# The current step's tap of a Mamba convolution moves from VectorE to ScalarE, which computes it with its bias out of PSUM, in a four-block decoder kernel on one core

## The chip, the cores and the metric

The kernel runs on one core of a Trainium2 chip. The metric is the device time of one launch in microseconds (us). A core has five engines that run programs of their own and wait for each other on semaphores: TensorE (PE in the profile, with its weight loads as PEld), VectorE (DVE), ScalarE (ACT), GpSimd (POOL) and SyncE (SP, which starts DMAs).

## The reference, cut to what matters

32 samples of 128 tokens and 256 features go through four blocks: an attention, a Mamba-2 block with a cross attention, a masked decoder layer and an attention with a feed-forward part. The change lies in the Mamba block's causal convolution of four taps over time, for each of 768 channels:

```python
zxbcdt = _rms(x, norm_w) @ in_proj_w
z = zxbcdt[..., :D_INNER]
xBC = zxbcdt[..., D_INNER:D_INNER + CONV_DIM]
...
padded = jnp.pad(xBC, ((0, 0), (D_CONV - 1, 0), (0, 0)))
conv = conv_b + sum((padded[:, k:k + L, :] * conv_w[:, k] for k in range(D_CONV)))
xBC = jax.nn.silu(conv)
```

Tap 3 is that of the current step: it reads the unshifted values.

## The kernel before, in words

One sample after another goes through a list of some 100 named tasks (xbc0, Q3, scores1, ...). Each engine has its own order of all tasks of all samples, sorted from a table of places written out by hand (TASKS, FIRST, LAST, SETUP, SHIFT), so that each engine works on up to five samples in turn: while one sample is in its Mamba block, others are in later attentions. "Xbc0 of sample 13" is written xbc0(13) here; samples count from 0. An engine never takes a later task while an earlier one waits.

Channels lie on the 128 partitions for the convolution: 768 channels are six chunks of 128 channels by 128 steps. The way of a sample through it:

- PE: the tasks xbc0 and xbc1 each project three chunks into one PSUM bank (in `xbc`, through `to_channels`, L639).
- ACT: `xbc` (L1104) copies the bank, 128x384, into the SBUF tile raw behind three columns of zeros, and then frees the bank.
- DVE: `convolve` (tasks conv0 and conv1) waits until the copy is done, then writes conv = raw x tap 3 + bias, three instructions (L1353), and adds taps 0, 1 and 2, nine instructions (L1358). Between taps it waits on a semaphore of its own (`step`), since each tap reads what the last one wrote.
- ACT: `convolved` (task silu, L1118) takes the tanh of conv/2 over all six chunks; DVE `silu` (L1364) gives x times sigmoid; PE `pairs` (L843, then transposes at L627) multiplies the B and C chunks and turns the others. DVE then scans (L1392), masks (L1396), and PE goes on in task Y (L858).

Four PSUM banks form a ring. Each PE task that writes one (a job: xbc0, x3T, mT4, K3, Q3 and so on) claims the next bank in PE's order: job number modulo 4. `claim` makes PE wait until the job four places earlier has been read, which the reading engine tells through bank_read. Another four banks, score, hold attention scores.

Around the convolution PE's order in most samples is: row(n-2), xbc0(n), x3T(n-2), mT4(n-3), quads1(n-1), K3(n-2), Q3(n-2), z1(n), xbc1(n), quads3(n-2), turn1(n-1), V3(n-2), e3(n-2), values1(n-1), ... , z0(n), values4(n-3), x2T(n-1), ld(n), quadsT3(n-2), pairs(n). Row, x3T, mT4, K3, Q3, z1 use the ring, quads1 does not. So xbc0's bank is the one that Q3 claims. ACT's order there is x3T (L1019), row (L1149), xbc0 (L1104), scores1 (eight exponentials, L1044), Q3 (L1025), z1 (L1111 to L1113), xbc1 (L1104), softplus (L1099), turn1 (two copies, L1057). DVE's is scores1 (L1249), K3 (L1465), conv0, scores3, e3, softplus (L1372 to L1374), finish1, n3, conv1, mT3 (L1269), Wo (L1432 to L1436), silu (L1364).

SPARE gives numbers of idle matmuls (L634) that PE runs ahead of some tasks of the first samples, where it would otherwise stand still. A spare one shows as two matmuls in the trace. ACT work with a scale or a bias that is a column of values, one for each partition, is `nc.scalar.activation(..., scale=..., bias=...)`.

Of the kernel before, what the change touches and what calls it, by code (L numbers as in the profile page):

```python
# [9 lines left out]
ALU = mybir.AluOpType  # L10
ACT = mybir.ActivationFunctionType
AX_X = mybir.AxisListType.X

P = 128
# [10 lines left out]
TAPS = 4  # L25
# [27 lines left out]
    back2=42.7145, back3=51.1225, back4=64.1374, conv0=15.1721, conv1=-1.5314, ctxT=34.1467, decayed=32.8056, down=71.1144,  # L53
# [20 lines left out]
    Y=(-0.1446, -0.2213, 0, -0.2465, 0, -0.2111, -0.4731, -0.2058), am=(-0.7507, 0, 0.1238, 0.0772, 0.1122, 0.0313, 0.0705, 0),  # L74
# [3 lines left out]
    back2=(-0.3118, -0.5887, -0.1007, 0.1753, 0.4363, 0.188, -0.0778, -0.0163),  # L78
# [17 lines left out]
    ld=(-1.9618, -0.6167, -0.8394, 0.0345, 0.9095, 0.0199, 0.0318, -0.0664),  # L96
    loadc=(-0.1305, -2.114, 0, -0.1491, 0, -0.1671, 0.0566, -1.6471),
    loadx=(-1.0589, 1.7209, 0.3386, -1.5237, 2.0519, -0.0978, 2.0094, -0.9573),
    mT2=(-0.2214, -0.039, 0, -0.1666, -0.0082, -0.1469, 0, 0), mT3=(0.1507, -0.0649, 0, 0.0742, 0.0046, -0.0294, -0.0199, 0),
    mT4=(0.0725, -0.0808, 0.0206, 0, 0.298, -0.0486, 0.0939, 0), n2=(0, -0.3557, 0, 0.1358, 0, 0.0553, -0.089, -0.9991),  # L100
    n3=(0.0571, 0.1417, 0.0077, 0, 0, 0.0336, -0.0298, -0.0179), norm2=(0, 0, 0.0986, 0.039, 0.0839, -0.1068, 0, -0.0236),
    norm3=(0.2169, 0, 0.1959, 0, -0.0031, 0, 0.0318, 0.324), norm4=(0.071, 0.0335, 0.32, -0.1077, 0.2364, -0.0289, 0.096, 0.0302),
    norm5=(0.0068, -0.3911, 0.0867, 0, 0.5488, -0.0845, 0, -0.0979),
    pairs=(-0.1812, 0.017, 0.1446, 0.0111, -0.0547, 0.0181, -0.0375, 0),
# [27 lines left out]
    xhatT=(-0.6957, 0.4202, 0.4868, 0, -0.2191, -0.364, 0.188, -0.0647),  # L132
    xnT=(-0.1522, 0, 0.002, -0.142, -0.1203, -0.0386, 0.273, -0.0477),
# [13 lines left out]
    back2=(0.1938, 0.0024, 0.135, -0.005, -0.0551, -0.2771), back3=(0.0375, -0.032, -0.245, -0.0948, 0.0736, 0.6035),  # L147
# [9 lines left out]
    ld=(0.0029, -0.2246, 0.1986, 0, 0.0376, 0.1683), loadc=(3.1754, 0, -0.3153, 0, 0, 0),  # L157
# [5 lines left out]
    pairs=(-0.0772, 0.1328, 0.0556, -0.01, 0.2526, 0.0232), proj=(0.0701, 0, -0.0083, 0.4015, 0, 0.3376),  # L163
# [9 lines left out]
    uT=(0, -0.1254, 0.2253, 0, -0.135, 0.0359), up0=(-0.1023, -0.0508, 0.2482, -0.1079, -0.8006, 27.5814),  # L173
# [8 lines left out]
    xnT=(0.032, -0.0811, 0.0628, -0.074, -0.0236, -0.0959), z0=(0.032, 0, -0.0425, 0.0328, 0, -0.0819),  # L182
# [8 lines left out]
    ACT=dict(  # L191
        K2=0.4275, K4=0.371, KE2=2.1051, KE3=-8.3627, Q1=0.2401, Q2=0.4113, Q3=0.0246, Q4=1.2096, V1=0.0661, V2=0.6553, V3=0.3112,
        Y=1.0681, attT2=-3.4331, attT3=31.0217, attT4=8.7138, ctxT=-0.4571, exps2=-6.4438, exps3=39.9244, exps4=40.2808,
        fc1=0.7372, ld=-0.1039, row=0.2044, scores1=-0.7902, silu=-0.1882, softplus=-0.2365, turn1=0.1793, uT=0.4762, up0=0.6797,
        up1=0.4246, x1=-0.5175, x2T=-0.0673, x3T=0.071, x4T=0.2522, x5T=0.318, x6T=0.3578, xbc0=0.1868, xbc1=0.439, xhatT=0.0635,
        xnT=0.9282, z0=0.0015, z1=0.2322, K0=-24.9607, Q0=-31.7526, V0=-0.7018, attT0=-21.6729, exps0=39.9731, prep_in=-3.1006),
# [11 lines left out]
        ld=8.6234, loadc=-5.0975, loadx=16.7863, spread=13.2176, store=78.055, load_mamba=-31.3063, load_w1=-56.8981,  # L208
# [26 lines left out]
PLACE_OF = {engine: {key: n for n, key in enumerate(order)} for engine, order in ORDER.items()}  # L235


SPARE = {("mT0", 0): 11, ("values0", 0): 9, ("back0", 0): 3, ("xhatT", 0): 6, ("ld", 0): 16, ("pairs", 0): 5, ("Y", 0): 18, ("uT", 0): 6, ("xnT", 0): 9, ("ctxT", 0): 10, ("x2T", 0): 7, ("Y", 1): 3, ("mT2", 0): 4, ("back2", 0): 3, ("n3", 0): 3}


RING_JOBS = dict(bias="bias0 bias1", pairs="CB xh", turn1="turn1_0 turn1_1")
# [162 lines left out]
def decoder_stack(nc, a, out):  # L404

    ctx = ExitStack()
    with ctx:
        def sb(name, shape, dt=F32):
            return ctx.enter_context(nc.sbuf_tensor(name, shape, dt))
# [29 lines left out]
        def vec(name):  # L439
            return vectors[:, VECTOR_AT[name]:VECTOR_AT[name] + VECTORS[name]]  # L440

        m_norm, g_norm, conv_b, ca_w, ca_b = (vec(n) for n in ("m_norm", "g_norm", "conv_b", "ca_w", "ca_b"))
        conv_w = vec("conv_w").rearrange("p (c k) -> p c k", c=XBC)
# [18 lines left out]
        raw = sb("raw", [P, 2, XBC, TAPS - 1 + P])  # L462
# [23 lines left out]
        conv = sb("conv", [P, 2, XBC, P])  # L486
        dbx, dx, zs, tz = (sb(n, [P, 2, INNER]) for n in ("dbx", "dx", "zs", "tz"))
        uT = tz[:, :, :].rearrange("p m (c k) -> p m c k", c=IC)
# [112 lines left out]
        def _(pe):  # L601
# [28 lines left out]
            def spare(it, what, lane, times):  # L630

                t, full = claim(it, what, lane)
                for _ in range(times):
                    mm(t[:, 0:P], ident, ident, start=True, stop=True)  # L634
# [363 lines left out]
            def program():  # L998
                for task, l, i in ORDER["PE"]:
                    if i == 0 and (task, l) in SPARE:  # L1000
                        spare(Of(i), RING_JOBS.get(task, task).split()[0], l, SPARE[task, l])
                    if task in do:
# [5 lines left out]
        def _(act):  # L1008
            run = nc.scalar.activation

            def filled(it, what, lane=0):

                b, use = job(it, what, lane)
                act.wait_ge(bank_full[b], use + 1)
                return bank[b], bank_read[b]
# [74 lines left out]
            def copied(what, n=D):  # L1090

                return lambda it, l: copy_out(it, what, l, actT[:, l], n)
# [8 lines left out]
            def xbc(it, l, half):  # L1101
                n = XBC // 2
                t, read = filled(it, f"xbc{half}", l)
                nc.scalar.copy(raw[:, l % 2, half * n:(half + 1) * n, TAPS - 1:],  # L1104
                               t[:, 0:n * P].rearrange("p (c k) -> p c k", c=n)).then_inc(read, 1)

            def z(it, l, half):
                n = INNER // 2
# [71 lines left out]
            def up(it, l, half):  # L1180
                t, read = filled(it, f"up{half}", l)
                for k in range(FC // 2):
# [7 lines left out]
                      ld=decays, Y=Y, uT=flip_u, xnT=copied("xnT"), Q1=Q1, x2T=copied("x2T"),  # L1190
                      Q2=Q2, K2=K_2, V2=V_2, x3T=copied("x3T"), row=row, Q3=Q3, V3=V3, x4T=copied("x4T"), fc1=fc1,
                      K4=K4, x5T=copied("x5T"), Q4=Q4, x6T=copied("x6T"),
                      **{f"{task}{half}": lambda it, l, f=f, half=half: f(it, l, half)
                         for task, f in (("xbc", xbc), ("z", z), ("up", up)) for half in range(2)},
                      x1=x1)
            do.update(scores1=exponential1, turn1=turned_out1, ctxT=copied("ctxT"))
# [12 lines left out]
        def _(dve):  # L1209
            tt, ts, stt = nc.vector.tensor_tensor, nc.vector.tensor_scalar, nc.vector.scalar_tensor_tensor  # L1210
# [7 lines left out]
            def evacuated(it, what, lane=0):  # L1218
                b, use = job(it, what, lane)
                dve.wait_ge(bank_read[b], use + 1)  # L1220
# [11 lines left out]
            def normalise(it, l, root, done):  # L1232
                dve.wait_ge(S[root], nth(it, l))
                ts(att[:, l, :], res[:, l, :], stat[:, l, 0:1], stat[:, l, 10:11],
                   ALU.subtract, ALU.mult).then_inc(S[done], 1)
# [62 lines left out]
            step = Chain(dve, S["dve_first"])  # L1298
# [9 lines left out]
            def program():  # L1308
                step = Chain(dve, S["dve_step"])
# [39 lines left out]
                def convolve(l, half):  # L1349
                    chunks = range(half * XBC // 2, (half + 1) * XBC // 2)  # L1350
                    evacuated(it, f"xbc{half}", l)
                    for c in chunks:
                        last = ts(conv[:, l % 2, c, :], raw[:, l % 2, c, TAPS - 1:], conv_w[:, c, TAPS - 1:TAPS],  # L1353
                                  conv_b[:, c:c + 1], ALU.mult, ALU.add)
                    for k in range(TAPS - 1):
                        step(last)
                        for c in chunks:
                            last = stt(conv[:, l % 2, c, :], raw[:, l % 2, c, k:k + P], conv_w[:, c, k:k + 1],  # L1358
                                       conv[:, l % 2, c, :], ALU.mult, ALU.add)
                    last.then_inc(S[f"conv{half}"], 1)  # L1360
# [119 lines left out]
                def down(l):  # L1480
# [4 lines left out]

                do = dict(finish0=lambda l: weighted(it, 0, l, step, att0[:, :]), prep_in=prep_in, prep_masks=prep_masks,
                          prep_out=prep_out, prep_q1=prep_q1, K1=K_1, softplus=softplus, conv0=lambda l: convolve(l, 0), conv1=lambda l: convolve(l, 1), silu=silu, pairs=pairs, scan=scan, decayed=decayed, Y=gate,
                          uT=gate_norm, proj=mamba_out, xnT=lambda l: normalise(it, l, "rstd3", "xn"),
                          
# [202 lines left out]
```

## Time and profile before

| | us |
|---|---|
| median of 3 runs | 1672.24 (1670.99 to 1676.52) |
| the profiled execution, whole | 1675.6 |
| its span, first to last instruction | 1673.8 |
| mean granted TensorE clock | 0.99 |
| busy: PE, PEld, DVE, ACT, POOL | 1616.5, 1393.2, 1387.1, 1039.8, 493.3 |

The profile is one execution. Its busy times are unions of an engine's instructions. In lines by group, the two numbers behind the bar are the busy time in us and the mean ns of one instruction, and after the second bar stands the idle time of the engine just before them, with what ended it. In a timeline a row is start, length, engine, line, operation, written tile and read tiles, shapes and count, and in brackets the idle time before it and what ended it. Consecutive instructions of an engine overlap by some 0.1 us in these records, so starts, not lengths, tell the rate.

### The profile page before, as it was taken

Reading aid. Unit: us, or ns where it says so; the run is one execution under the profiler, and the core shown is the slowest. Engines: PE = TensorE matmul, PEld = TensorE weight load, DVE = VectorE, ACT = ScalarE, POOL = GpSimd, SP = SyncE. Lnnn points to the kernel's source line nnn. Section 1 sums busy time; section 2 is a strip of 40 time slices with the busy share of each in tenths; the row PEclk is TensorE's granted clock in tenths of the full one; section 3 lists DMA queues with packets and bytes.
Section 4 is the critical chain, followed back from the end, with each engine's and each line's share of the span. In section 5 each row is a group of like instructions: output and inputs, shape, how many; then the busy total and the mean of one; then the engine's idle time right before and its main releaser. Section 6 shows DMA issues by size and latency. Waiting matters only on the chain.

```text
span 1673.8 us, 61139 instructions
## 1 busy us (share of the span) xinstructions
PE 1616.5 (97%) x25060; PEld 1393.2 (83%) x25060; DVE 1387.1 (83%) x3585; ACT 1039.8 (62%) x2667; POOL 493.3 (29%) x1256
## 2 busy tenths in 40 slices
PE   7899999999999999999999999999999999999986
PEld 6777888888888888888888888888888888888774
DVE  4689888888888889888888988888898888898652
ACT  2355666766666676666667666666766666676652
POOL 2333223333322332332233233223323322333110
PEclk9999999999999999999999999999999999999997
DMA  6110000000000000000000000000000000000000
GB/s 216 52 64 21 6 18 31 18 25 28 22 3 24 25 24 24 25 17 9 24 25 25 25 24 22 5 24 25 24 25 24 17 10 24 21 28 19 5 5 7
DMA packets 31316, 44.37 MB, mean 27 GB/s; under 512 B 3008, under 2 KB 26176, under 8 KB 30912
## 3 DMA queue, kind: packets, MB, share of 16 engines
q1 hardware_dynamic: 31040, 40.45, 7.4%
q8 instruction: 202, 3.31, 0.8%
q14 instruction: 74, 0.61, 0.1%
HBM read 36.12 MB, written 4.33 MB: 24 GB/s over the span
## 4 chain that ended last, share of the span: by engine, by line
PE 55%; DVE 36%; issue 5%; POOL 2%; DMA 1%; ACT 1%; SPq 0%; DVEq 0%; POOLq 0%; ACTq 0%
PE ring L639 18%; PE ring L645 14%; PE ring L627 6%; DVE conv L1358 5%; DVE maxima_at L1258 5%; PE score L707 4%; DVE decay L1392 4%; PE score L731 3%; PE ring L773 3%; DVE decay L1396 2%; PE ring L858 2%; DVE conv L1364 2%; DVE QB L1269 2%; DVE conv L1353 2%; PE score L671 2%
## 5 line engine op out<-in xcount | busy, mean ns | idle before, releaser
L1533 POOL TENSOR_TENSOR stat<-stat 128x1 f32<-128x1 f32 x224 | 131.7, 594 | 617.2 <-DVE stat L1224 616.6
L1019 ACT COPY actT<-ring 128x256 f32<-128x256 f32 x256 | 95.5, 373 | 291.7 <-PE ring L627 290.5
L1258 DVE TENSOR_REDUCE maxima_at<-score 128x4 f32<-128x512 f32 x388 | 240.8, 684 | 25.5 <-PE score L707 24.5
L1052 ACT ACTIVATE weights<-score 128x512 f32<-128x512 f32 x388 | 200.7, 607 | 28.5 <-PE score L731 27.9
L1358 DVE SCALAR_TENSOR_TENSOR conv<-raw,vectors,conv 128x128 f32<-128x128 f32 x576 | 169.0, 349 | 6.8
L639 PE MATMUL ring<-actT,w_q 128*128 128x128 f32 x1024 | 141.5, 281 | 0.7 <-ACT actT L1019 0.7
L639 PEld LDWEIGHTS ring<-actT,w_q 128*128 128x128 f32 x1024 | 124.5, 191 | 12.8 <-issue 11.3
L639 PE MATMUL ring<-actT,w_up 128*128 128x128 f32 x1024 | 129.6, 281 | 0.5 <-ACT actT L1019 0.5
L639 PEld LDWEIGHTS ring<-actT,w_up 128*128 128x128 f32 x1024 | 121.1, 194 | 3.7 <-ACT actT L1019 1.1
L1184 ACT ACTIVATE gT<-ring,vectors 128x128 f32<-128x128 f32 x256 | 73.0, 368 | 72.2 <-PE ring L639 71.5
L645 PE MATMUL ring<-w_down,gT 128*128 128x256 f32 x512 | 115.9, 379 | 1.3 <-issue 1.3
L731 PE MATMUL score<-QB,KE 32*128 32x128 f32 x3104 | 115.9, 286 | 1.0 <-DVE QB L1269 1.0
L731 PEld LDWEIGHTS score<-QB,KE 32*128 32x128 f32 x3104 | 97.1, 189 | 20.7 <-issue 16.6
L773 PE MATMUL ring<-weights,V 128*32 128x128 f32 x3104 | 106.9, 278 | 3.4 <-issue 3.3
L645 PEld LDWEIGHTS ring<-w_down,gT 128*128 128x128 f32 x512 | 94.9, 190 | 13.0 <-issue 1.4
L639 PE MATMUL ring<-cT,w_k 128*128 128x128 f32 x768 | 104.4, 279 | 0.0
L1269 DVE SCALAR_TENSOR_TENSOR QB<-ring,const,QB 128x256 f32<-128x256 f32 x194 | 84.5, 477 | 20.4 <-PE ring L627 20.3
L1063 ACT COPY attT<-ring 128x512 f32<-128x512 f32 x97 | 56.2, 579 | 72.7 <-PE ring L773 72.6
L645 PE MATMUL ring<-w_v,cT 128*128 128x256 f32 x384 | 100.3, 384 | 0.4 <-ACT V L1036 0.4
L773 PEld LDWEIGHTS ring<-weights,V 128*32 128x32 f32 x3104 | 80.5, 111 | 23.8 <-issue 10.1
L639 PEld LDWEIGHTS ring<-cT,w_k 128*128 128x128 f32 x768 | 95.4, 191 | 4.9 <-issue 0.2
L639 PE MATMUL ring<-actT,w_in 128*128 128x128 f32 x768 | 98.7, 279 | 0.7 <-DVE q_bias L1337 0.7
(179 smaller groups left out, 3814.8 us busy)
## 6 DMA issues: line engine op xcount, KB each, us to landing
decay<-rates_out SPq DMA_DIRECT2D x32, 512.0 KB, 3.9
cT<-in_ctxT SPq DMA_DIRECT2D x32, 128.0 KB, 2.2
x_in<-in_x SPq DMA_DIRECT2D x32, 128.0 KB, 2.4
out<-result SPq DMA_DIRECT2D x32, 128.0 KB, 2.1
row_all<-in_rows SPq DMA_DIRECT2D x1, 1420.0 KB, 9.9
w_in<-in_in_proj SPq DMA_DIRECT2D x1, 1288.0 KB, 7.2
w_k<-in_k SPq DMA_DIRECT2D x4, 256.0 KB, 5.8
w_v<-in_v SPq DMA_DIRECT2D x4, 256.0 KB, 5.7
```

The source lines that it names most:

```text
L627: last = nc.tensor.transpose(t[:, c * P:(c + 1) * P], src[:, c * P:(c + 1) * P], ident)
L639: last = mm(t[:, at:at + P], w[:, c, cols:cols + P], xT[:, c, :], start=(c == 0), stop=(c == n - 1))
L645: last = mm(t[:, at:at + hi - lo], xT[:, c, :], w[:, c, lo:hi], start=(c == 0), stop=(c == n - 1))
L731: last = mm(score[:, r, at:at + P], KE[rows_of, l, c, e, :], QB[rows_of, l, c, e, :], start=(not masked and at == 0), stop=(c == DC - 1 an ...
L773: last = mm(output[ROWS_OF[r], four * P:(four + 1) * P], V2[:, l, h, :], weights[:, buffer, h % 8 // 2, at:at + P], start=True, stop=True)
L1019: nc.scalar.copy(dst.rearrange("p c k -> p (c k)"), t[:, 0:n]).then_inc(read, 1)
L1052: run(weights[:, turned_buffer(it, a_, l), r, :], score[:, r, :], ACT.Exp).then_inc(S["exps"], 1)
L1184: last = run(gT[:, l % 2, c, :], t[:, k * P:(k + 1) * P], ACT.Gelu, bias=up_b[:, c:c + 1])
L1258: nc.vector.tensor_reduce(maxima_at[:, maxima_buffer(it, a_, l), :, 32 * r:32 * r + 17:16], score[:, r, :].rearrange("p (c f k) -> p c f k ...
L1269: last = stt(QB[:, l, :, e, :], t[:, 0:D].rearrange("p (c k) -> p c k", c=DC), spare_row[:, e:e + 1], QB[:, l, :, e, :], ALU.mult, ALU.add)
L1358: last = stt(conv[:, l % 2, c, :], raw[:, l % 2, c, k:k + P], conv_w[:, c, k:k + 1], conv[:, l % 2, c, :], ALU.mult, ALU.add)
L1533: tt(stat[:, l, 10:11], stat[:, l, 2:3], stat[:, l, 4:5], ALU.pow).then_inc(S[done], 1)
```

## The change

ACT still copies the bank into raw. Before it frees the bank it now also computes tap 3 with its bias, with three ACTIVATEs (Identity, scale and bias both columns) for each half, from the PSUM bank straight into conv. Only the last of them frees the bank. DVE's three instructions for tap 3 are gone, and the first wait on its own semaphore with them. All engine orders are kept. Five spare matmuls of the first sample are taken away: one ahead of ld(0), four ahead of ctxT(0).

```diff
-SPARE = {... ("ld", 0): 16, ... ("ctxT", 0): 10, ...}
+SPARE = {... ("ld", 0): 15, ... ("ctxT", 0): 6, ...}
...
                 nc.scalar.copy(raw[:, l % 2, half * n:(half + 1) * n, TAPS - 1:],
-                               t[:, 0:n * P].rearrange("p (c k) -> p c k", c=n)).then_inc(read, 1)
+                               t[:, 0:n * P].rearrange("p (c k) -> p c k", c=n))
+                for k in range(n):
+                    c = half * n + k
+                    last = run(conv[:, l % 2, c, :], t[:, k * P:(k + 1) * P], ACT.Identity,
+                               scale=conv_w[:, c, TAPS - 1:TAPS], bias=conv_b[:, c:c + 1])
+                last.then_inc(read, 1)
...
                     evacuated(it, f"xbc{half}", l)
-                    for c in chunks:
-                        last = ts(conv[:, l % 2, c, :], raw[:, l % 2, c, TAPS - 1:], conv_w[:, c, TAPS - 1:TAPS],
-                                  conv_b[:, c:c + 1], ALU.mult, ALU.add)
                     for k in range(TAPS - 1):
-                        step(last)
+                        if k:
+                            step(last)
                         for c in chunks:
```

## Rows read from the trace of the kernel before

**Rows 1.** The page's first part: busy time of each engine

```profile
PE 1616.5 (97%) x25060; PEld 1393.2 (83%) x25060; DVE 1387.1 (83%) x3585; ACT 1039.8 (62%) x2667; POOL 493.3 (29%) x1256
```

**Rows 2.** Busy us (count) of PE, PEld, DVE, ACT, POOL; clock; DMA

```profile
600.00:700.00 100.00, 99.13 (x1580) 85.78 (x1581) 87.72 (x225) 65.61 (x171) 32.47 (x82) 1.00 0.07 21
```

**Rows 3.** Groups by line: the removed DVE work, the nearest ACT form

```profile
L1353 DVE TENSOR_SCALAR conv<-raw,vectors 128x128 f32<-128x128 f32 x192 | 54.5, 341 | 1.5 <-ACT raw L1104 1.5
L1176 ACT ACTIVATE QB<-ring,q_bias,const 128x128 f32<-128x128 f32 x128 | 48.3, 463 | 2.5 <-PE ring L639 2.5
```

**Rows 4.** Timeline of ACT: a train of four, then around xbc0(13) and xbc1(13)

```profile
626.39 1.51 ACT L1176 ACTIVATE QB<-ring,q_bias,const 128x128 f32<-128x128 f32 x4
...
634.41 0.37 ACT L1019 COPY actT<-ring 128x256 f32<-128x256 f32 x1 [1.04 <-PE ring L627]
...
634.83 0.50 ACT L1104 COPY raw<-ring 128x384 f32<-128x384 f32 x1
636.15 2.17 ACT L1044 ACTIVATE exps<-score,neg_max 128x128 f32<-128x128 f32 x8 [0.82 <-DVE neg_max L1249]
...
639.51 0.53 ACT L1104 COPY raw<-ring 128x384 f32<-128x384 f32 x1
640.64 0.21 ACT L1099 ACTIVATE dts<-dts 128x8 f32<-128x8 f32 x1 [0.61 <-POOL dts L1550]
641.20 0.59 ACT L1057 COPY weights<-ring 128x512 f32<-128x512 f32 x1 [0.35 <-PE ring L627]
```

**Rows 5.** Timeline of PE and of its weight loads: Q3(11) behind K3(11)

```profile
636.18 1.06 PE L639 MATMUL ring<-actT,w_q 128*128 128x128 f32 x8
...
636.08 0.97 PEld L639 LDWEIGHTS ring<-actT,w_q 128*128 128x128 f32 x8
```

**Rows 6.** Xbc0's copy of samples 9 and 31, and Q3 behind the last (window's end)

```profile
438.83 0.50 ACT L1104 COPY raw<-ring 128x384 f32<-128x384 f32 x1
...
1516.89 0.50 ACT L1104 COPY raw<-ring 128x384 f32<-128x384 f32 x1
...
1518.24 0.50 PE L639 MATMUL ring<-actT,w_q 128*128 128x128 f32 x3
```

**Rows 7.** Timeline of DVE and ACT: conv1(13), tanh, silu(13)

```profile
644.41 0.85 DVE L1353 TENSOR_SCALAR conv<-raw,vectors 128x128 f32<-128x128 f32 x3
...
648.09 0.85 ACT L1118 ACTIVATE raw<-conv 128x768 f32<-128x768 f32 x1
...
649.79 1.10 DVE L1364 SCALAR_TENSOR_TENSOR conv<-raw,conv 128x768 f32<-128x768 f32 x1
```

**Rows 8.** Weight loads: pairs(13), turn1(12) behind quads3(11), and waits of 150:1550

```profile
650.95 0.30 PEld L843 LDWEIGHTS ring<-conv 128*128 128x128 f32 x2 [0.27 <-DVE conv L1364]
...
640.06 0.32 PEld L707 LDWEIGHTS score<-K,QB 32*128 32x128 f32 x8
640.50 0.86 PEld L627 LDWEIGHTS ring<-const,exps 128*128 128x128 f32 x8
...
PEld ring L843 <- DVE conv L1364: 8.0, 27, 0.6
```

**Rows 9.** Timeline of ACT and PE: xbc1(5)'s copy and what follows, values1(4)

```profile
247.47 0.53 ACT L1104 COPY raw<-ring 128x384 f32<-128x384 f32 x1
247.84 1.13 ACT L1069 ACTIVATE KE<-K,const 128x256 f32<-128x256 f32 x2
...
249.16 1.07 ACT L1057 COPY weights<-ring 128x512 f32<-128x512 f32 x2
...
250.50 0.83 PE L750 MATMUL ring<-V,weights 128*32 128x33 f32 x64
```

**Rows 10.** The start: conv0(0) on DVE, softplus(1) on ACT

```profile
33.54 0.86 DVE L1353 TENSOR_SCALAR conv<-raw,vectors 128x128 f32<-128x128 f32 x3 [1.49 <-ACT raw L1104]
...
67.93 0.21 ACT L1099 ACTIVATE dts<-dts 128x8 f32<-128x8 f32 x1 [0.22 <-POOL dts L1550]
```

More of the change, by code:

```diff
@@ L235 @@
 PLACE_OF = {engine: {key: n for n, key in enumerate(order)} for engine, order in ORDER.items()}
-SPARE = {("mT0", 0): 11, ("values0", 0): 9, ("back0", 0): 3, ("xhatT", 0): 6, ("ld", 0): 16, ("pairs", 0): 5, ("Y", 0): 18, ("uT", 0): 6, ("xnT", 0): 9, ("ctxT", 0): 10, ("x2T", 0): 7, ("Y", 1): 3, ("mT2", 0): 4, ("back2", 0): 3, ("n3", 0): 3}
+SPARE = {("mT0", 0): 11, ("values0", 0): 9, ("back0", 0): 3, ("xhatT", 0): 6, ("ld", 0): 15, ("pairs", 0): 5, ("Y", 0): 18, ("uT", 0): 6, ("xnT", 0): 9, ("ctxT", 0): 6, ("x2T", 0): 7, ("Y", 1): 3, ("mT2", 0): 4, ("back2", 0): 3, ("n3", 0): 3}
 RING_JOBS = dict(bias="bias0 bias1", pairs="CB xh", turn1="turn1_0 turn1_1")
```

## The prediction, made before the changed kernel was run

> **What bounds the kernel now.** I read the shares of the engines first, then the stretches, then the waits of PE, and last the timeline around one sample. The page shows PE 97% busy and DVE 83%, ACT 62% [rows 1]. A share over the whole span hides two regimes, so the stretches come next: in the first 150 us PE stands idle a good part of the time (its digits in the page's slices are 7 to 9), from then to about 1550 us it is busy 99 us of every 100 [rows 2]. In that long middle nothing that DVE or ACT saves can count unless PE waits for it, and anything that makes PE wait costs its full length, since PE has no idle time left to make it up. A sample takes 49.0 us there: the copies of xbc0(9) and xbc0(31) start 22 periods apart, (1516.89 - 438.83) / 22 [rows 6]. So the question is not how much work moves but which PE waits shrink and which appear.
>
> **The change part by part.**
>
> *DVE loses three instructions a half.* A trio takes 0.85 us [rows 7], and 192 of them are 54.5 us of DVE [rows 3]. At conv0 the gain is worth nothing: the next DVE task, scores3, waits for scores whose last weight loads end only at 640.38 [rows 8], when conv0 used to be nearly done anyway. At conv1 it counts partly: mT3 behind it waits for PE's transposes, and then Wo and silu follow. I take 0.55 us of the 0.85, an estimate. The tanh stands in between: it starts at 648.09, right when conv1 is done, and ends at 648.94, while silu starts at 649.79 [rows 7]. So silu may move by up to 0.85 us even with the tanh where it is, and 0.55 us fits. Who waits for silu: PE's pairs. Its weight load stood idle 0.27 us for DVE, and so it did 27 times in the middle for 8.0 us in all [rows 8]. Not all of this comes back. Behind a task of narrow 32-row matmuls PEld pauses without any wait: turn1's load starts at 640.50 where quads3's end at 640.06 + 0.32 = 640.38, a pause of 0.12 us [rows 8]. Pairs too comes behind such a task, so its gain is 0.27 - 0.12 = 0.15 us. Over 28 samples that is 4.2 us, and the few samples with a longer wait (0.6 us at most [rows 8]) give perhaps 0.9 us more: **-5.1 us**. Its bounds are 0, if the tanh or another DVE task comes late, and -8.0 us, the whole row.
>
> *ACT gains three ACTIVATEs a half, ahead of the release of the bank.* The nearest form is L1176: 128x128 fp32 out of PSUM, scale and bias both columns, 463 ns each [rows 3], and four of them take 1.51 us [rows 4], so one starts (1.51 - 0.46) / 3 = 0.35 us after the other. The work is 192 x 0.35 = 67 us more on ACT, from 62% to 66% of the span: no bound by itself. But the bank of xbc0 is released late. The copy starts at 634.83 and ends at 635.33. With three ACTIVATEs behind it, the first 0.37 us after the copy's start (as the next instruction follows the copy of xbc1(5), 247.84 - 247.47 [rows 9]), the last ends at 634.83 + 0.37 + 0.70 + 0.46 = 636.36. Next on that bank is Q3, four ring jobs on, and its first weight load starts at 636.08 [rows 5]. A load starts about 0.06 us after its release, as that of pairs(13) at 650.95 behind silu's end at 650.89 [rows 7, 8]. So it comes at 636.42, 0.34 us late. This is PE waiting for ACT where it waited for nothing. And it comes back every sample, because ACT cannot start xbc0's copy earlier: it comes behind x3T and row, which wait for PE [rows 4]. The distance from the copy's end to Q3's first matmul (636.18 - 635.33) is 0.85 us in nineteen samples (9 to 25, 27 and 31, of which 13 stands in [rows 4, 5] and the last in [rows 6]). Nineteen times 0.34 is **+6.5 us**. Three more samples (3, 8, 28) have distances of 0.6 to 1.1 us against the 0.85 + 0.34 = 1.19 us needed: 0.1, 0.2 and 0.5 us, **+0.8 us**. The other ten have 1.4 us or more or the bank goes to a later job.
>
> Here the Trainium skill has a price of its own, the page "ScalarE: Activation LUTs", section "What ACT_TABLE_LOAD costs": an ACTIVATE takes 186 ns and 0.833 ns for each element of a row, each pointer operand adds 93 ns, and two in a row overlap by 93 ns. For 128 elements and two pointers that is an estimate of 479 ns, one every 386 ns; rows 3 and 4 have 463 and 350, so the trace is lower, and the row decides. By the page's figures the stall would be 2 x 0.036 + 0.016 = 0.09 us longer and the sum 1.7 us higher.
>
> *What is queued behind the new work on ACT.* Behind xbc0: the exponentials of scores1, which waited 0.82 us for DVE anyway and now start 0.1 us later; PE's turn1 needs them 2.2 us after their end (636.15 + 2.17 against 640.50 [rows 4, 8]). Behind xbc1: softplus and turn1, with 0.61 and 0.35 us of idle time ahead of them [rows 4], 0.96 us against 1.03 us of new work (634.83 + 0.50 to 636.36), and Q3's stall has moved PE by 0.34 us as well, so turn1 waits for PE as before: nothing. In samples 5, 6 and 30 these two have no such idle time. There turn1's copies end at 250.23 and values1 starts at 250.50 [rows 9]. I take half of the 0.27 us for slack and the rest for the way of a release, and 0.1 us of ACT's idle time besides, so of the 1.03 us some 0.8 us reach PE: 0.8 us each for 5 and 30, 0.7 us for 6, and, read in the same way, 0.8 us in all for V3 and values1 at samples 4, 28 and 29: **+3.1 us**. Bounds of this term: 0 and +6 us, if most regular samples also lose 0.1 us.
>
> *The start.* Conv0(0) starts right when ACT has copied, at 33.54 [rows 10]. The last of ACT's three ends near 34.6, where DVE's tap 0 began at 34.4 (33.54 + 0.86): conv0 comes 0.2 us later, conv1 behind it keeps 0.85 us, so pairs(0) is some 0.7 us earlier. One sample on, this is mostly lost: xbc1(1) stands ahead of softplus(1) on ACT, with 0.22 us of idle time [rows 10], so DVE's softplus and the chain of POOL, ld and the DMA for the decays behind it move by about +0.6 us. **-0.3 us**, between -1.5 and +1.5. The spare matmuls taken out (10 of the trace's matmuls at 0.12 us, 1.2 us) lie where PE waits for other engines: nothing. Each sat in front of a wait, and values1(0) comes up to 0.9 us later, which eats into the wait that the four ahead of ctxT(0) filled.
>
> **Sum.** -5.1 + 6.5 + 0.8 + 3.1 - 0.3 = +5.0 us. The profiled execution took 1675.6 us whole, so it would take 1680.6. It is 3.4 us above the median of the runs, and I carry the difference over to the median: 1672.2 + 5.0 = **1677.2 us**, +0.30%. A measurement of this kernel can tell about 0.3% (5.0 us: below 1667.2 or above 1677.3) from no change. This forecast is a small loss that lies on the upper of these bounds.
>
> **The rivals.**
>
> *A. DVE's relief counts and the bank does not stall PE.* It holds if ACT's three end before 636.02, that is if they add 0.69 us and not 1.03 us. Against it: L1176's rate. For it: only that no row shows this very instruction. Then both stall terms are 0.4 in place of 7.3, and pairs brings its upper bound: -8.0 + 0.4 + 3.1 - 0.3 = -4.8, near 1667.
>
> *B. The stall comes and the relief doesn't: slower.* One mechanism: pairs stays held because silu's tanh is behind ACT's queue, which now is longer. It decides when the tanh, against PE, starts later than 648.09 + 0.85 - 0.15 = 648.8, since its end then leaves nothing of pairs' 0.15 us [rows 7]. For it: 1.03 us of new work stands ahead of it twice. Against it: ACT waits for PE at ctxT between turn1 and the tanh, and starts afresh there. The sum is then +5.0 + 5.1 = +10.1: 1682.3.
>
> *C. Nothing moves.* The work on both engines lies beside PE's, and the stall at Q3 is taken back by later waits of PE in the same sample (Y for DVE's decay among them). Against it: these waits follow from chains that start at a PE task behind Q3, so they move along. 1672.
>
> **How the numbers follow.** The forecast's case (both the stall and part of the relief, 1673 to 1681) has 0.55, A 0.12, B 0.20, C 0.13. Within the forecast's case the bound of 0.3% divides almost in the middle. Faster by over 0.3%: two thirds of A, 0.08. Slower by over 0.3%: half of 0.55, less a little for stalls that I may have counted too high, 0.25, and B's 0.20, 0.45. Within: 0.47. For the range, the term of pairs goes from 0 to -8.0, that of the irregular samples from 0 to +6, the start by 1.5 either way; they are independent, and 1668 to 1684 leaves out most of A and the far end of B.
>
> **What would show each step.** In the changed kernel's trace: 192 ACTIVATEs at the new line with a mean near 460 ns and starts 0.35 us apart; the weight load of Q3 waiting some 0.3 us for ACT about nineteen times (6 us); the load of pairs no longer waiting for DVE's silu; DVE near 1333 us and ACT near 1107 us busy; and the period of a sample 49.1 to 49.2 us where it was 49.0. The prediction is wrong if Q3's load does not wait, if the pairs' wait stays, or if a wait of over 0.1 us a sample shows up at values1, V3 or quads1 in the regular samples.

## The result and the profile after

| | before | after |
|---|---|---|
| median, us | 1672.89 (4 runs, 1670.99 to 1676.52) | 1697.93 (4 runs, 1697.26 to 1698.58) |
| the profiled execution, whole | 1675.6 | 1697.26 |
| its span | 1673.8 | 1695.4 |

The changed kernel takes 1.0147 times as long (95% interval 1.0129 to 1.0165): 25 us more by the medians, 21.6 us by the two profiled spans, where +5.0 was forecast. Busy times first, which answer to [rows 1], and a stretch of the middle, which answers to [rows 2]:

```profile
PE 1621.2 (96%) x25050; PEld 1394.1 (82%) x25050; DVE 1331.8 (79%) x3393; ACT 1103.9 (65%) x2859; POOL 494.8 (29%) x1256
...
600.00:700.00 100.00, 97.80 (x1545) 84.47 (x1545) 82.27 (x211) 68.58 (x178) 30.95 (x78) 1.00 0.06 21
```

The work moved as announced: DVE lost 55.3 us, ACT gained 64.1 us, and PE runs the same instructions, but for the spare ones, at the same granted clock (1.00 in this stretch before and after). But PE is now idle 2.2 us of the 100 where it was idle 0.87 us. The period of a sample went from 49.00 us [rows 6] to (1538.66 - 438.46) / 22 = 50.01 us, by the same two copies in the timeline of ACT:

```profile
438.46 0.50 ACT L1104 COPY raw<-ring 128x384 f32<-128x384 f32 x1
...
1538.66 0.50 ACT L1104 COPY raw<-ring 128x384 f32<-128x384 f32 x1
```

PE's program is the same but for the spare matmuls, so the loss can be laid out by task: how much later, against the end of PE's task before it, each task ends in the changed kernel than in the one before, over 32 samples.

| task of PE | us | |
|---|---|---|
| ld | +18.9 | 0.93 to 0.98 in eighteen samples, 0.5 to 0.6 in four: 3, 8, 21 and 27 |
| Q3 | +8.0 | 0.42 in each of nineteen samples |
| values1, V3 | +2.9 | values1 0.6 at samples 4, 5, 28, 29; V3 0.4 in two |
| pairs | -7.7 | of it -2.96 at sample 0, and -0.15 in most others |
| all others | 0.0 | between -1.9 (x2T) and +1.6 (values3), they cancel |
| sum | +22.1 | |

The two spans differ by 0.5 us less, since the first task ends that much earlier in the changed kernel.

So the forecast's stall, its relief and its irregular samples are all there, and one item of 19 us stands beside them of which the forecast had nothing: ld, the small task between x2T and pairs that spreads the log decay over the steps. The view of the waits names what it waits for (us in all, times, the longest):

```profile
PEld ring L849 <- POOL dts L1581: 23.8, 25, 1.1
PE ring L849 <- POOL dts L1581: 17.3, 22, 0.8
PE ring L639 <- ACT conv L1108: 3.9, 20, 0.3
PE ring L750 <- ACT weights L1057: 2.9, 5, 0.8
PEld ring L843 <- DVE conv L1367: 1.4, 4, 0.7
```

The first two lines are new; in the kernel before they were small:

```profile
PEld ring L849 <- POOL dts L1578: 2.1, 4, 0.6
...
PE ring L849 <- POOL dts L1578: 0.7, 3, 0.3
```

The last line, pairs waiting for silu, was 11.2 us in 29 waits over the whole span of the kernel before. In the stretch of [rows 8], 150 to 1550 us, the 8.0 us in 27 waits became 0.5 us in 2: pairs hardly waits for silu any more. What ld now waits for is one GpSimd instruction of 128x8 elements, the product of the step sizes with the decay rates ("the log decay" below). Its rows by line, before and after (shortest, median and longest, in ns):

```profile
L1578 POOL TENSOR_TENSOR dts<-dts,row_all x32: 201/202/305, 37.5 to 1531.5; 128x8 f32<-128x8 f32 x32
```
```profile
L1581 POOL TENSOR_TENSOR dts<-dts,row_all x32: 201/944/1022, 37.5 to 1553.7; 128x8 f32<-128x8 f32 x32
```

GpSimd's instruction was not touched, and it got five times as long. The timelines around sample 13 show beside what. The kernel before, GpSimd:

```profile
649.24 0.20 POOL L1578 TENSOR_TENSOR dts<-dts,row_all 128x8 f32<-128x8 f32 x1 [0.18 <-POOL dts L1566]
649.46 0.62 POOL L1593 TENSOR_TENSOR V<-V,keep 128x256 f32<-128x256 f32 x1
650.14 0.82 POOL L1595 COPY V<-keep 128x16 f32<-128x16 f32 x1
```

The changed kernel, GpSimd, VectorE and PE:

```profile
654.31 1.02 POOL L1581 TENSOR_TENSOR dts<-dts,row_all 128x8 f32<-128x8 f32 x1 [0.18 <-ACT tz L1118]
655.29 0.61 POOL L1596 TENSOR_TENSOR V<-V,keep 128x256 f32<-128x256 f32 x1
655.97 0.21 POOL L1598 COPY V<-keep 128x16 f32<-128x16 f32 x1
...
654.31 0.96 DVE L1367 SCALAR_TENSOR_TENSOR conv<-raw,conv 128x768 f32<-128x768 f32 x1
...
655.38 0.27 PE L849 MATMUL ring<-const,dts 128*8 128x128 f32 x1 [0.82 <-POOL dts L1581]
655.59 1.17 PE L731 MATMUL score<-QB,KE 32*128 32x128 f32 x32
656.69 0.49 PE L843 MATMUL ring<-conv 128*128 128x128 f32 x2
```

Before, silu started at 649.79 [rows 7], 0.55 us behind the log decay. In the changed kernel both start at 654.31, and the log decay ends at 655.33, 0.06 us after silu's end at 655.27. The same holds wherever it starts with or inside silu, in 22 samples: it always ends 0.06 us behind silu. In sample 26 it starts 0.01 us ahead of silu instead; there it takes 0.20 us, and silu takes 1.00. Silu did hold a GpSimd instruction in the kernel before too: the 128x16 copy at L1595 took 0.82 us where it takes 0.21 us when nothing lies beside it (median 0.214 us of its 64). Nobody waited for that copy. The change moved silu off an instruction that nobody needs onto one that PE needs at once. Against the start of PE's xbc1, silu of sample 13 begins 0.51 us sooner than before and the log decay 0.04 us later, together the 0.55 us that lay between them.

**Theory P**, so named in the expectations: silu, with its two inputs in SBUF, locks GpSimd out of reading SBUF until it ends. **Q**, the rival: ld waits because of the work added to ScalarE for the first half, which frees a bank late and pushes what is queued behind it; then ld's wait should come and go with that half. The Trainium skill states such a lock in "SBUF — State Buffer", section "Who interferes with whom": a VectorE instruction with two SBUF inputs and a GpSimd instruction that reads SBUF exclude each other for a whole instruction, and the one that issues first wins. By that rule the trace agrees; the experiments below try it.

### The profile page after: what moved, and what is told of

Same layout as the page of the kernel before. It is cut to its first block, busy times and chain, and to the rows that moved or that the text cites. A ratio compares the mean times of both kernels' runs of the same rounds, so it can differ in the third digit from the quotient of the medians.

```text
span 1695.4 us, 61119 instructions
## 1 busy us (share of the span) xinstructions
PE 1621.2 (96%) x25050; PEld 1394.1 (82%) x25050; DVE 1331.8 (79%) x3393; ACT 1103.9 (65%) x2859; POOL 494.8 (29%) x1256
## 4 chain that ended last, share of the span: by engine, by line
PE 76%; ACT 9%; DVE 7%; POOL 4%; issue 3%; DMA 1%; SPq 0%; DVEq 0%; POOLq 0%; ACTq 0%
PE ring L639 25%; PE ring L645 18%; PE ring L627 9%; PE score L731 6%; PE score L707 5%; PE ring L773 4%; PE score L671 3%; PE ring L858 2%; ACT conv L1108 2%; DVE maxima_at L1263 2%; ACT weights L1052 1%; POOL dts L1581 1%; ACT actT L1019 1%; ACT exps L1044 1%; PE ring L750 1%
## 5 line engine op out<-in xcount | busy, mean ns | idle before, releaser
L1361 DVE SCALAR_TENSOR_TENSOR conv<-raw,vectors,conv 128x128 f32<-128x128 f32 x576 | 168.6, 348 | 6.7 <-ACT conv L1108 2.2
```

## The experiments

### One half at a time

Only the second half's tap (xbc1, conv1) goes to ScalarE:

```diff
-                for k in range(n):
+                for k in range(n if half == 1 else 0):
...
+                    if half != 1:
+                        for c in chunks:
+                            last = ts(conv[:, l % 2, c, :], raw[:, l % 2, c, TAPS - 1:], ...)
```

> Only the second half (xbc1, conv1) is computed by ScalarE; the first half is as in the kernel before. Theory P (port): the loss comes from VectorE's silu, which now starts early enough to hold the SBUF read port while GpSimd's log decay (a 128x8 product, 0.2 us) wants to run; ld waits for it. The early start comes from conv1 alone, so the stall of ld stays, about 19 us, the bank of xbc0 is released early again (8 us less than the changed kernel), pairs keeps its gain of 5 us, values1 keeps its loss of 3: 1673 + 19 - 5 + 3 = about 1690 us. Rival Q (queue): the log decay is late because ScalarE's longer queue and PE's wait at Q3 push the chain behind softplus; without xbc0's part most of it goes: about 1673 us.

And only the first half's (the same edit with 0 for 1):

> Only the first half (xbc0, conv0) is computed by ScalarE. Theory P: conv1 and silu keep their old time, so the log decay stays at 0.2 us and ld does not wait; only the release of xbc0's bank is late, 0.42 us at Q3 in nineteen samples: 1673 + 8 - 1 (start) = about 1680 us. Rival Q: the pushed queue is there, ld waits for most of its 19 us as in the changed kernel: about 1695 us.

Each ratio here and below is to runs of the kernel before taken beside it. The columns behind the median are the ledger's, against the profiled executions, in us.

| | ratio to before | median | ld | Q3 | pairs |
|---|---|---|---|---|---|
| second half only | 1.0084 (1.0065 to 1.0104) | 1687.87 | +19.0 | 0 | -7.9 |
| first half only | 1.0058 (1.0041 to 1.0075) | 1683.14 | +0.7 | +8.0 | -0.5 |

The two costs part cleanly. The first half brings the stall of Q3 and little else. The second half brings the relief of pairs and the wait of ld with it, without any work added ahead of Q3. (Its 19.0 us are not spread as the changed kernel's are: 2.6 us lie at samples 0 and 1, and samples 7, 10, 13 and 19, where the log decay comes first, have no wait.) Q, which had 1673 for the second half alone and 1695 for the first alone, falls. The second half's waits look like the changed kernel's:

```profile
PEld ring L849 <- POOL dts L1585: 23.8, 24, 1.9
PE ring L849 <- POOL dts L1585: 17.7, 21, 1.8
```

### The log decay one instruction earlier

GpSimd computes the log decay ahead of an instruction that it does not need, 0.42 us sooner, so that it is over when silu starts:

```diff
                     step(tt(d(10), d(9), d(3), ALU.add))
+                    tt(d(5), d(10), decay_rate, ALU.mult).then_inc(S["am"], 1)
                     ts(d(11) ...
-                    tt(dts[:, 5, l, :], dts[:, 10, l, :], decay_rate, ALU.mult).then_inc(S["am"], 1)
```

> The changed kernel, with GpSimd's log decay computed one instruction earlier, before dt is halved (its input is ready then), so it starts 0.42 us earlier than now, 0.4 us ahead of silu. Theory P: it ends before silu takes the port, takes 0.2 us again, and ld's stall goes whole, though only 0.4 us were moved: 1698 - 19 = about 1679 us. Rival Q: a chain that is merely late gains what was moved, 0.42 us in each of some 20 samples: 1698 - 8 = about 1690 us.

Measured: 1681.96, ratio 1.0049 (1.0033 to 1.0064). Ld went to -2.6 us, below the kernel before; Q3 (+8.0), pairs (-6.9) and values1 (+2.4) stayed. P's 1679 is 3 us low, Q's 1690 is out. The timeline of sample 13 shows the lock gone to the next GpSimd instruction, for which PE does not wait:

```profile
648.87 0.20 POOL L1569 TENSOR_TENSOR dts<-dts,row_all 128x8 f32<-128x8 f32 x1
649.16 0.24 POOL L1570 TENSOR_SCALAR dts<-dts 128x8 f32<-128x8 f32 x1
649.36 1.37 POOL L1596 TENSOR_TENSOR V<-V,keep 128x256 f32<-128x256 f32 x1
...
649.29 0.96 DVE L1367 SCALAR_TENSOR_TENSOR conv<-raw,conv 128x768 f32<-128x768 f32 x1
```

L1596 takes 0.62 us alone. Here it starts 0.07 us into silu and takes 1.37.

### Silu later, silu in two

Three idle steps of one element ahead of silu move it behind the log decay, as it stood before:

```diff
                 def silu(l):
+                    for _ in range(3):
+                        step(ts(idle[:, 0:1], idle[:, 1:2], 1.0, None, ALU.mult))
                     dve.wait_ge(S["tanh"], nth(it, l))
```

> The changed kernel, with three idle steps of VectorE on one column each (about 0.6 us) ahead of silu, which puts silu back to its old place behind Wo. Theory P: although VectorE does more work, the log decay runs ahead of silu in 0.2 us again, ld's 19 us go, and pairs waits for silu as before the change, 5 us: 1698 - 19 + 5 = about 1684 us. Rival Q: nothing in ScalarE's or GpSimd's queue changes, the stall of ld stays, and pairs may get its wait back: 1698 to 1703 us.

Measured: 1689.01, ratio 1.0092 (1.0076 to 1.0109); its profiled run was 1685.2. In the trace the log decay is back at 0.20 us everywhere but one sample (0.31). Ld keeps +5.2 us, of it 2.5 at samples 0 and 1 (with the second half alone these two have 2.6, so the steps are not the reason), and pairs has only -1.6 left. The mechanism is P's; the time is 5 us above P's 1684 by the median, and 1 us by the profiled run. That difference between its own runs I cannot explain.

Silu in two instructions of 384 elements a row:

```diff
-                    stt(conv[:, l % 2, :, :], raw[...], 1.0, conv[:, l % 2, :, :], ...)
+                    w = XBC // 2
+                    for part in range(2):
+                        last = stt(conv[:, l % 2, part * w:(part + 1) * w, :], ...)
```

> The changed kernel with VectorE's silu in two instructions of 128x384 instead of one of 128x768. Theory P (port): the log decay that meets it waits only for the first half, so it takes about 0.5 us where it took 1.02, and ld waits about 0.45 us where it waited 0.93: in twenty samples 1698 - 9 = about 1689 us. Rival D: the log decay is delayed by any VectorE work at that moment, or waits for silu's result; then it lasts until the end of both halves, 1.1 us, and the time is 1698 to 1700 us.

Measured: 1683.54, ratio 1.0072 (1.0056 to 1.0087), 5.5 us better than P's 1689. The log decay took at most 0.62 us, half as with the whole silu, which is the lock's size: in samples 9 and 10 it starts with the first part and ends with it. But in only six samples was it 0.57 to 0.62; in most it started 0.01 us ahead of silu and took 0.20 us. Here the lock was a tie decided by some 10 ns, which P had not counted.

### Silu with one input in SBUF

The test that bears on P itself: the same element count and place in every order, but another reading pattern. The product of x and its sigmoid is left out in both kernels.

```diff
-                    stt(conv[:, l % 2, :, :], raw[...], 1.0, conv[:, l % 2, :, :], ALU.add, ALU.mult)
+                    nc.vector.tensor_reduce(conv[:, l % 2, :, :], raw[...].unsqueeze(3), AX_X, op=ALU.max)
```

> The changed kernel, with VectorE's product of x and its sigmoid (task silu, 128x768, two inputs in SBUF) left out and a reduction over an axis of length one in its place: the same number of elements, the same place in every order, but one input in SBUF, so the output is not the reference's. Theory P (GpSimd's log decay is locked out because VectorE's instruction has two inputs in SBUF): the log decay takes 0.20 us in every sample although the reduction starts at the same instant, ld does not wait, and the profiled span is near 1695.4 - 18.9 = 1676.5 us or up to 5 us above, if the reduction is longer than 0.96 us and pairs waits for it again. Rival E (any long VectorE instruction that starts at that instant holds the log decay up): it takes 1.0 us as in the changed kernel, ld keeps its 18.9 us and the span is near 1695.

```diff
+                    ts(conv[:, l % 2, :, :], raw[...], 1.0, 0.5, ALU.add, ALU.mult)
```

> The changed kernel, with the same product left out and a TENSOR_SCALAR of 128x768 in its place (one input in SBUF, two constants), so the output is not the reference's. If only the number of inputs in SBUF matters, the log decay takes 0.20 us and the span is near 1676. The Trainium skill, page 'SBUF — State Buffer', section 'Who interferes with whom', states a second case, a VectorE instruction in a mode that reads through both of its ports; by it a TENSOR_SCALAR in such a mode locks the log decay out as well, for its own length. The rows of before have 128x128 TENSOR_SCALARs at 341 ns and no 128x768 one, so its length is open: between 0.5 and 0.96 us, an estimate. If it locks, the log decay takes that length, ld waits 0.1 us less than it in some 20 samples, 8 to 17 us in all, and the span is near 1685 to 1694.

With the reduction (span 1678.0; 1679.81 whole, one run, beside 1669.01 for the kernel before) sample 8, where the log decay starts 0.34 us inside the reduction, and sample 13 read:

```profile
402.80 0.20 POOL L1581 TENSOR_TENSOR dts<-dts,row_all 128x8 f32<-128x8 f32 x1 [0.18 <-ACT tz L1118]
...
402.45 0.95 DVE L1367 TENSOR_REDUCE conv<-raw 128x768 f32<-128x768 f32 x1
...
649.96 0.20 POOL L1581 TENSOR_TENSOR dts<-dts,row_all 128x8 f32<-128x8 f32 x1 [0.18 <-ACT tz L1118]
650.18 0.62 POOL L1596 TENSOR_TENSOR V<-V,keep 128x256 f32<-128x256 f32 x1
650.87 0.21 POOL L1598 COPY V<-keep 128x16 f32<-128x16 f32 x1
...
649.97 0.95 DVE L1367 TENSOR_REDUCE conv<-raw 128x768 f32<-128x768 f32 x1
```

VectorE's instruction is as long as silu (0.95 against 0.96), and the GpSimd instructions run beside it at their own lengths. In 21 samples the log decay starts between 0.01 us ahead and 0.34 us inside the reduction, and it takes 0.20 us in all of them. Most of these prove little by themselves: in thirteen, sample 13 among them, it starts some 0.01 us ahead, where it could also have won the port. What decides are the six samples in which it starts 0.15 to 0.34 us inside, the 23 in which L1596 starts inside the reduction and takes its 0.62 us, and the reductions, which take 0.95 us in all 32 samples. Ld is at +2.5 (0.1 us a sample; x2T ahead of it is at -1.9) and pairs at -7.6, as P had it, and the span falls in P's 1676.5 to 1681.5. This total is the weaker part: against the kernel before that ran beside it (span 1667.1) it is 10.9 us, and each is a single run. The rival, that any long VectorE instruction there would do it, is gone.

With the TENSOR_SCALAR (span 1685.5; 1687.39 whole, one run) two samples show both outcomes of the tie, 11 first and 13 behind it:

```profile
551.92 0.62 POOL L1580 TENSOR_TENSOR dts<-dts,row_all 128x8 f32<-128x8 f32 x1 [0.18 <-ACT tz L1118]
...
551.93 0.56 DVE L1367 TENSOR_SCALAR conv<-raw 128x768 f32<-128x768 f32 x1
...
651.10 0.20 POOL L1580 TENSOR_TENSOR dts<-dts,row_all 128x8 f32<-128x8 f32 x1 [0.18 <-ACT tz L1118]
651.32 0.87 POOL L1595 TENSOR_TENSOR V<-V,keep 128x256 f32<-128x256 f32 x1
...
651.11 0.60 DVE L1367 TENSOR_SCALAR conv<-raw 128x768 f32<-128x768 f32 x1
```

It does 768 elements a row in 0.56 us where the reduction takes 0.95, and it locks although it has one input: in eleven samples the log decay ends 0.05 to 0.06 us behind it, and in eleven others it slipped in first and the TENSOR_SCALAR took 0.60 instead. So "two inputs in SBUF" is not the only form that locks. The Trainium skill, in the same section of "SBUF — State Buffer", names the second one: an instruction in a mode that uses both of VectorE's ports. The trace agrees so far as this one is faster, 0.56 against 0.95 us, and locks. Ld was +5.5 us, under the 8 to 17 expected: of the sixteen samples in which the two started within about 0.01 us of each other, the log decay went first in eleven. The span of 1685.5 lies at the expected 1685 to 1694 all the same, for reasons that lie in other tasks of that one run.

### What the repair is worth

The kernel before with only the log decay moved, the second half alone with it, and the changed kernel with it and with the bank freed right behind the copy (the tap then reads raw, which the copy has filled):

```diff
                 nc.scalar.copy(raw[:, l % 2, half * n:(half + 1) * n, TAPS - 1:],
-                               t[:, 0:n * P]...)
+                               t[:, 0:n * P]...).then_inc(read, 1)
+                evacuated(it, f"xbc{half}", l)
...
-                    last = run(conv[:, l % 2, c, :], t[:, k * P:(k + 1) * P], ACT.Identity,
+                    last = run(conv[:, l % 2, c, :], raw[:, l % 2, c, TAPS - 1:], ACT.Identity,
...
-                last.then_inc(read, 1)
+                last.then_inc(S[f"tap{half}"], 1)
...
-                    evacuated(it, f"xbc{half}", l)
+                    dve.wait_ge(S[f"tap{half}"], nth(it, l))
```

> The kernel before with the early log decay alone. There it did not meet silu, so only ld's small wait of 0.05 us a sample and some longer ones at samples 21 and 27 can go: -2 to -3 us, about 1670 us; the wait of pairs for silu stays. If the log decay's place were worth much by itself, without the port, it would show here as more than 5 us.

> Only the second half by ScalarE, and the early log decay. No late release at Q3, no wait for the port; left are the gain of pairs (about 7 us against the kernel before, with the start) and the losses at values1, V3 and turn1 (4 us): about 1671 us, a little below the kernel before. If VectorE's relief were worth nothing, 1677 us.

> The changed kernel with the early log decay, and the banks of xbc0 and xbc1 freed right behind the copy: ScalarE waits for its own copy and reads the tap's values from raw. If Q3's 0.42 us in nineteen samples is the late release of xbc0's bank, it goes although ScalarE does the same three ACTIVATEs: 1682 - 8 = about 1674 us. If ScalarE's longer queue itself delays what Q3 needs, it stays: 1682 us or more.

| | ratio to before | median | ld | Q3 | pairs | values1 |
|---|---|---|---|---|---|---|
| before, log decay early | 0.9978 (0.9969 to 0.9988) | 1668.86 | -2.4 | 0 | -2.9 | 0 |
| second half, early | 0.9996 (0.9987 to 1.0005) | 1670.87 | -2.7 | 0 | -7.3 | +2.5 |
| both halves, early, bank freed | 1.0012 (1.0003 to 1.0021) | 1673.36 | -2.7 | +0.7 | -4.3 | +8.2 |

All three came near what was expected (1670, 1671 and 1674). In the last the stall of Q3 is gone, +0.7 us, but what ScalarE's longer stretch costs came back at values1. Pairs gains 3.0 us less than in the row above, 2.7 of it at sample 0, and in twelve samples (13 to 23 and 25) silu takes 1.39 to 1.40 us where it takes 0.96 alone. The best kernel of the study is the one without the change at all: kernel before, log decay earlier. It gains twice. Ld loses its few waits, since the log decay is simply sooner (it took 0.20 us in nearly all samples before as well), and the drop of V (L1593) no longer stands in silu's way, which is the port. In sample 13 the kernel before has L1593 from 649.46 to 650.08 (above), and silu, which started 0.29 us ahead of its end, took 1.10 us [rows 7]. In the new kernel the drop comes sooner, only 0.13 us of it lie over silu, and silu takes 0.96:

```profile
646.97 0.62 POOL L1593 TENSOR_TENSOR V<-V,keep 128x256 f32<-128x256 f32 x1
...
647.46 0.96 DVE L1364 SCALAR_TENSOR_TENSOR conv<-raw,conv 128x768 f32<-128x768 f32 x1
```

Pairs gains 0.1 us a sample there.

## Why the prediction was wrong, step by step

**The step that failed** is in the part on DVE's lost instructions. It moved silu 0.55 us ahead and asked only who waits for silu, not what silu would run beside. The text read a gain of 0.55 us off rows of DVE, ACT and PE; GpSimd's timeline was not among them. It would have shown the log decay starting 0.55 us ahead of silu, with ld waiting for it at once, and a 128x16 copy under silu at 0.82 us where it takes 0.21. The two 0.55 are the same distance, and the shift ended exactly on it. That the estimate of 0.55 us came out so near (0.51 measured) was good judgement; that the log decay stood at just that place was bad luck, but it could be read. That cost +18.9 of the ledger's +22.1 us. Without it the ledger would stand at +3.2, against the sum of +5.0. None of the rivals held it, and the upper end of 1684 was missed by 14 us.

**Pairs**: -0.15 us a sample was forecast from a wait of 0.27 less a pause of 0.12, and the ledger has -0.15 in most samples. Without sample 0 it is -4.7 us against -5.1. Right. The tanh did not hold silu, so rival B's mechanism is absent (its 1682 was on the right side, for another reason).

**Q3**: a stall in nineteen samples was forecast, and the same nineteen have it (named there by the copy's sample, which is two above Q3's). Right in place, but 0.42 us each and not 0.34: +8.0 for +6.5. Here is sample 13, to be held beside [rows 4, 5]:

```profile
639.45 0.50 ACT L1104 COPY raw<-ring 128x384 f32<-128x384 f32 x1
639.82 1.18 ACT L1108 ACTIVATE conv<-ring,vectors 128x128 f32<-128x128 f32 x3
...
641.14 1.13 PE L639 MATMUL ring<-actT,w_q 128*128 128x128 f32 x8 [0.19 <-ACT conv L1108]
```

From the copy's start to Q3's first matmul it was 1.35 us and is 1.69: 0.34, as worked out. The other 0.07 lie behind it: the eight matmuls take 1.13 us where they took 1.06. I read this as the overlap that PE loses when it stops (the first load has no matmul before it to run under). No run tried it apart, and it was not in the sum. The single ACTIVATE measured 479 ns on average (median 469, from 457 to 567):

```profile
L1108 ACT ACTIVATE conv<-ring,vectors 128x128 f32<-128x128 f32 x192 | 75.5, 479 | 0.0
```

The Trainium skill's figures ("ScalarE: Activation LUTs", "What ACT_TABLE_LOAD costs") gave an estimate of 479 for one, which is this mean. For the pace they gave 386 ns; here three take 1.18 us, (1.18 - 0.48) / 2 = 0.35 us apart, which is the row's pace. The page was nearer on the length, the trace on the pace, and the pace made the stall.

**Irregular samples**: +3.1 forecast, +2.9 measured in values1 and V3, and in the places named. The prediction counts by the sample n of xbc1; the tasks of PE that its late end reaches are values1(n-1), which waits for turn1's copies, and V3(n-2), which in samples 4 and 28 has the bank of xbc1. Its samples 5, 6 and 30 are values1(4), (5) and (29): 0.66, 0.56 and 0.66 us for 0.8, 0.7 and 0.8. Its samples 4, 28 and 29 are V3(2), V3(26) and values1(28): 1.3 us for 0.8. A 0.3 us gain at values1(0) makes up the rest. So the sum was right by an excess and a shortfall that cancel. Of the 0.8 us for three more samples of the bank's late release one part came: 0.6 us at K3(26), which has the bank of xbc0(28), for the 0.5 forecast. The other two (0.1 and 0.2) did not appear.

**The start**: -0.3 forecast. Pairs(0) came 2.96 us earlier instead of 0.7, and some of it was kept: xbc0(9) starts 0.37 us earlier than before (438.46 against 438.83) although ld and values1 had cost PE 3.3 us by then. Silu(0) started 1.49 us earlier (40.48 for 41.97), and it took 0.96 us instead of 1.68: before, a GpSimd product (L1573, from 41.57 on) had started ahead of it. Mis-sized, to the good, and partly by the same lock.

**Turn1 and softplus**: nothing in regular samples, as said.

## What to carry to other kernels

When a change moves an instruction of VectorE, read what GpSimd runs at the new place, and who waits for that: a gain of some tenths of a us can set two engines onto one port at the point where a third waits. A GpSimd instruction whose longest duration is several times its median is the sign, and it can be read before any change. The repair is to move the short instruction that somebody waits for ahead of the long one, which here was free and worth 0.2% by itself.

## What the runs showed of the hardware

- While silu, a VectorE instruction with two SBUF inputs, runs, a GpSimd instruction that starts with it or inside it does not end before it, however small: 128x8 elements took 1.02 us instead of 0.20, 128x16 took 0.82 instead of 0.21, 128x256 took 1.37 instead of 0.62. All of these read and write SBUF; no run tells which of the two is held.
- With one of VectorE's two inputs in PSUM there was no such hold, and the kernel before shows it: in 28 samples GpSimd's L1566 starts 0.11 us inside L1432 and takes 0.24 us and ends before it. So does L1565 ahead of it, at its 0.20 us, beside L1269, which is a SCALAR_TENSOR_TENSOR like silu but has one input in PSUM.

```profile
648.71 0.41 DVE L1432 TENSOR_TENSOR res<-ring,res 128x256 f32<-128x256 f32 x1
648.82 0.24 POOL L1566 TENSOR_SCALAR dts<-dts 128x8 f32<-128x8 f32 x1
```

- It goes the other way as well: silu took 1.42 us instead of 0.96 in sample 4 of the changed kernel, where GpSimd's L1596 had started 0.01 us ahead of it (the delay of 0.46 us is the overlap of 0.61 less 0.15; by the same 0.15 the overlaps of 0.29 and 0.13 us above make 0.14 and nothing). GpSimd's loss follows the same sum to 0.01 us: 0.82 us for an overlap of 0.96 at the log decay, 0.75 for 0.89 at L1596 in the kernel with the early log decay.

```profile
206.65 0.62 POOL L1596 TENSOR_TENSOR V<-V,keep 128x256 f32<-128x256 f32 x1
...
206.66 1.42 DVE L1367 SCALAR_TENSOR_TENSOR conv<-raw,conv 128x768 f32<-128x768 f32 x1
```

- A TENSOR_REDUCE of the same 768 elements a row held neither the log decay, in six samples where that started 0.15 to 0.34 us inside it, nor L1596, in 23. A TENSOR_SCALAR with one input, fp32 in SBUF to SBUF at 0.56 us, does lock.
- Some 0.01 us decided who waited. With the TENSOR_SCALAR the log decay went first in eleven samples, where it started 0.005 to 0.012 us ahead, and waited in five, where it started 0.001 to 0.005 us ahead; so the cost of such a tie cannot be told from a mean. Nor is the edge at the same place for every instruction: in the changed kernel GpSimd instructions that started up to 0.02 us inside a 128x128 tap of the convolution (L1361) still took their usual 0.20 or 0.24 us (in sample 13 one of 0.20 us at 649.46, the tap running from 649.44 on).
